# One half of the scan's decay in SBUF, a sixth PSUM bank in the ring, and the feed-forward layer's norms and first weights inside the last attention unit

## What is computed

```python
def _L0_attn_ref(x, ...):
    xn = _ln(x, ln1_w, ln1_b)
    q, k, v = heads of xn @ q_w + q_b, xn @ k_w + k_b, xn @ v_w + v_b     # 16 heads of 8
    attn = softmax(where(causal, q k^T * hd ** -0.5, -inf))
    attn_out = (attn v) @ o_w + o_b
    x_ssm, z = split(xn @ in_proj_w)                                      # 256 channels each
    x_c = silu(conv4(x_ssm) + conv_b)
    dt, Bm, Cm = softplus(x_dbc[..., :R] @ dt_w + dt_b), ...              # 16 states
    h_t = exp(dt_t * A) * h_(t-1) + (x_t * dt_t) * B_t;  y_t = sum_n C_t h_t
    ssm_out = ((y + x_c * D_param) * silu(z)) @ ssm_out_w
    x = x + alpha * attn_out + (1 - alpha) * ssm_out
    h2 = _ln(x, ln2_w, ln2_b)
    return x + gelu(h2 @ ffn_w1 + ffn_b1) @ ffn_w2 + ffn_b2
```

## Time and profile before

| | |
|---|---|
| median of 3 runs | 1673.72 us (1668.92 to 1680.34) |
| the profiled execution | 1669.76 us |
| its span, first to last instruction | 1668.0 us |
| mean granted TensorE clock | 0.934 of full speed |
| PE, DVE, ACT, POOL busy | 84%, 76%, 66%, 52% of the span |
| attention with SSM | 130 to 845 us, then unit 15 alone to 877 |
| norms `ln2` and first weights | 877 to 903 us |
| feed-forward layer | 903 to 961 us |

### The profile page before, as it was taken

How to read it: one execution, slowest core, us unless ns; L and a number is a source line. 1 busy time by engine, 2 the same in 40 slices (tenths; PEclk the granted TensorE clock), 3 DMA queues, 4 the chain that set the end, 5 groups by cost and what they waited for, 6 DMA issues and landing times. The chain is left out here.

```text
span 1668.0 us, 22123 instructions
## 1 busy us (share of the span) xinstructions
PE 1408.5 (84%) x7164; PEld 884.0 (53%) x7164; DVE 1261.6 (76%) x1873; ACT 1093.5 (66%) x1864; POOL 863.4 (52%) x889
## 2 busy tenths in 40 slices
PE   3688898888989898887767887999999999868687
PEld 3234444444444444444324645787786877725573
DVE  2149999989798988989915858687686767848857
ACT  2475668686767778786746736777878788621017
POOL 3137677778696978878843113022222222248843
PEclk9787899999999999999988989999999999979889
DMA  3112222222222222222003010111111111000001
GB/s 90 45 39 83 77 63 78 80 75 70 64 68 67 78 73 68 80 76 75 27 1 95 19 48 26 33 48 45 40 49 39 45 45 45 26 0 1 0 1 50
DMA packets 61688, 84.73 MB, mean 51 GB/s; under 512 B 6621, under 2 KB 32071, under 8 KB 61575
## 3 DMA queue, kind: packets, MB, share of 16 engines
q1 hardware_dynamic: 61474, 83.30, 16.0%
q10 hardware_dynamic: 100, 0.03, 0.0%
HBM read 74.38 MB, written 8.78 MB: 50 GB/s over the span
## 5 line engine op out<-in xcount | busy, mean ns | idle before, releaser
L1760 POOL TENSOR_TENSOR dBx<-dtx,Bb 128x512 f32<-128x512 f32 x256 | 319.6, 1272 | 11.4 <-DMA Bb<-b_dram 10.1
L1355 DVE TENSOR_TENSOR hl<-lsq,hh 128x512 fp32r<-128x512 f32 x320 | 259.5, 821 | 86.7 <-ACT hh L1644 78.9
L1325 DVE TENSOR_TENSOR_SCAN hy<-bank,dBx 128x512 f32<-128x512 f32 x256 | 297.8, 1203 | 10.5 <-ACT bank L1628 6.0
L1641 ACT ACTIVATE lsq<-bank,vcol 128x512 f32<-128x512 f32 x320 | 219.4, 692 | 108.1 <-DVE hl L1355 61.0
L1050 PE MATMUL bank<-QK 127*128 127x128 bf16 (+7 forms) x1024 | 237.7, 318 | 46.6 <-DVE Mx L1315 27.9
L1315 DVE TENSOR_REDUCE Mx<-bank 128x1 f32<-128x384 f32 (+3 forms) x352 | 212.1, 627 | 57.5 <-PE bank L1050 56.7
L1784 POOL TENSOR_TENSOR stage<-stage,lrs 128x512 f32<-128x512 f32 x64 | 92.3, 1443 | 310.5 <-DVE lrs L1435 310.5
L1050 PE MATMUL bank<-x,we1h 128*128 128x512 f32 x640 | 210.7, 411 | 18.8 <-DVE x L1343 9.4
L1569 ACT ACTIVATE PT<-bank 128x512 f32<-128x512 f32 x320 | 183.7, 596 | 52.9 <-PE bank L1050 51.3
L1628 ACT ACTIVATE bank<-dtv,alog 128x512 f32<-128x512 f32 x256 | 170.4, 692 | 61.2 <-DVE hy L1325 60.8
L1050 PEld LDWEIGHTS bank<-QK 127*128 127x128 bf16 (+1 forms) x1024 | 94.3, 104 | 191.9 <-issue 51.5
(11 more groups left out here) (258 smaller groups left out, 2393.6 us busy)
## 6 DMA issues: line engine op xcount, KB each, us to landing
Bb<-b_dram SPq DMA_DIRECT2D x128, 256.0 KB, 3.6
stage<-w_rows SPq DMA_DIRECT2D x64, 256.0 KB, 3.2
parts<-part SPq DMA_DIRECT2D x16, 384.0 KB, 2.7
QK<-parts SPq DMA_DIRECT2D x64, 96.0 KB
QK<-parts SPq DMA_DIRECT2D x64, 64.0 KB
stage<-in_L_ffn_We_dram SPq DMA_DIRECT2D x16, 256.0 KB, 3.3
hy<-in_L_attn_x_dram SPq DMA_DIRECT2D x8, 256.0 KB, 5.8
QK<-parts SPq DMA_DIRECT2D x64, 32.0 KB
```

The source lines that it names most:

```text
L1325: engine.tensor_tensor_scan(hst[:, 2 * (g % 3) + h, :], bank[4 + h][:], dBx[:, g % 4, h, :], 0.0, ALU.mult, ALU.add).then_inc(sems["dve_sc ...
L1355: engine.tensor_tensor(hl[:, sl, :], full[:, f, :], hh[:, sl, :].bitcast(F32), ALU.subtract).then_inc(sems["dve_hl"], 1)
L1641: engine.activation(full[:, f, :], o[:], fn, bias=bias).then_inc(sems["act_up"], 1)
L1760: engine.tensor_tensor(dBx[:, sl, h], dtx[:, b % 2, h], Bb[:, sl], ALU.mult).then_inc(sems["pool_dbx"], 1)
```

## The change

- **Decay.** The decay of half 0 is written to `dec = On[:, 1, :]` in SBUF; half 1 stays in bank 5. The attention's `On` shrinks to one tile, `On[:, 0, :]`, so that `on` of one half batch waits for `wo` of the one before.
- **Ring.** It becomes `[0, 1, 2, 4, 6, 7]`.
- **Accumulation.** `BESIDE` no longer holds for the last batch.
- **Last unit.** `second_norms` and `plan_ffn`, now a generator, are moved on within unit 15 at 16 and 20 steps to its 20. The norm of batch 7 waits until the layer has reached block `LAST_NORM = 4`. The squares of `ln2` go to `part` instead of `lsq`. The first weights and x wait for the end of the SSM branch alone (`ends["ssm"]`); for this the tiles of that branch are allocated first, and the four weight tiles become one, `wall`, with expert 9 in front. The weights of experts 8, 0, 1 and 2 wait for the end of the attention and are split in blocks 2 to 5 (before: 0 to 3).
- **Experts.** In the feed-forward layer `up` takes its banks from the ring and `down` takes 4 and 5. The DVE cast for c = 2 now also holds for e = 9.

```diff
+LAST_NORM = 4
-    ring = [0, 1, 2, 6, 7]
@@ decay, scan
-        it = step("decay", g=g, dt=ssm[b]["dt"], free=[free.get(f"b{4 + h}") for h in range(2)])
+        it = step("decay", g=g, dt=ssm[b]["dt"], free=(free.get("dec"), free.get("b5")))
...
-            free[f"b{4 + h}"] = free[f"dBx{g % 4}{h}"] = it["x"][h]
+            free[("dec", "b5")[h]] = free[f"dBx{g % 4}{h}"] = it["x"][h]
@@ accumulate
-                      y_free=free.get("yT"), y_last=ssm[b]["y"][half], beside=b >= 2 and n in BESIDE, yb_free=free.get(f"yB{half}", nT_read))
+                      y_free=free.get("yT"), y_last=ssm[b]["y"][half], beside=2 <= b < NB - 1 and n in BESIDE, yb_free=free.get(f"yB{half}", nT_read))
@@ plan_mixers
+    def second_norms():
+        for b in range(NB):
+            while ended[b] < 2 or b == NB - 1 and ends.get("ffn", 0) < LAST_NORM:
+                yield
+            k = take()
+            ring.remove(k)
+            finish_norm = p.norm_start((k, ring[0]), (h_last[b],), kind="ln2", b=b, square="part", dst_free=(free.get("yB0"), free.get("yB1")) if b < 2 else None)
+            for _ in range(2):
+                yield
+            r_h2[b] = finish_norm()
+            ring.append(k)
+            yield
...
     for u in range(NU):
-        run_together(attend(u), 20, (mixer, SSM_RATE, False), (tops, 23, False), (prepare(u), 8, True))
+        last = 1 if u == NU - 1 else 0
+        run_together(attend(u), 20, (mixer, SSM_RATE, False), (tops, 23, False), (prepare(u), 8, True),
+                     (seconds, 16 * last, False), (behind_it, 20 * last, False))
+    drain(mixer)
     while late or later:
         settle(0)
-    drain(mixer)
+        next(seconds, None)
+        next(behind_it, None)
+    ends["att"] = tuple(p.last.values())
+    ring.append(3)
+    for _ in behind_it:
+        next(seconds, None)
@@ Experts
+        k = p.first_free(self.ring) if self.ring else c
...
-        if c == 2 and e < 9:
+        if c == 2:
             it["y"] = p.up("dve_hh")
@@ plan_ffn
-    drain(p.norms([(r_h2, b, (bk[b % 4], (h_last[b], *done)), dict(kind="ln2", b=b)) for b in range(NB)]))
-    x.split_weights(0, 9, done)
+    while "ssm" not in ends:
+        yield
+    x.split_weights(0, 9, ends["ssm"])
     load_x(0)
-    x.split(0, r_h2[0], done)
+    while not r_h2[0]:
+        yield
+    x.split(0, r_h2[0], ends["ssm"])
+    while "on" not in ends or 4 not in ring:
+        yield
+    ring.remove(4)
@@ vector_program, scalar_program
-                        engine.tensor_tensor_scan(hst[:, 2 * (g % 3) + h, :], bank[4 + h][:], dBx[:, g % 4, h, :], 0.0,
+                        engine.tensor_tensor_scan(hst[:, 2 * (g % 3) + h, :], bank[5][:] if h else dec, dBx[:, g % 4, h, :], 0.0,
...
-                        engine.activation(bank[4 + h][:], dtv[:, b % 2, h, :], ACT.Exp,
+                        engine.activation(bank[5][:] if h else dec, dtv[:, b % 2, h, :], ACT.Exp,
```

More of the change, by code:

```diff
@@ L244, in normalise @@
         k = take()
-        it = step("on", b=b, g=g, o1=o1, bank=k, free=free.get(f"b{k}"), lrs_free=free.get(f"lrs{hf}"), on_free=free.get(f"On{hf}"))
+        it = step("on", b=b, g=g, o1=o1, bank=k, free=free.get(f"b{k}"), lrs_free=free.get(f"lrs{hf}"), on_free=free.get("On"))
         it["m"] = up("pe_dn")
@@ L462, in mamba @@
         drain(behind)
+        ends["ssm"] = tuple(p.last.values())
     def prepare(u):
@@ L487, in plan_mixers @@
     fetch(0)
[L488 removed]
+    for k in (0, 1, 2, 4):
         ring.remove(k)
     run_together(p.norms(first_norms([(1, 1)] + [(b, l) for l in range(2) for b in range(2, NB)])), 12, (mixer, 5, False))
[L491 removed]
+    ring.extend((0, 1, 2, 4))
     fetch(1)
@@ L507, in __init__ @@
     def __init__(self, p):
-        self.p, self.queue, self.n, self.split_done, self.w_done, self.slots = p, [], 0, {}, {}, {}
+        self.p, self.queue, self.n, self.split_done, self.w_done = p, [], 0, {}, {}
+        self.ring, self.down = None, 6
     def split(self, b, ready, done=()):
@@ L580, in load_x @@
     def load_x(b):
-        it = step("x2load", b=b, free=free.get(f"xin2{b % 2}"), done=done)
+        it = step("x2load", b=b, free=free.get(f"xin2{b % 2}"), done=ends["ssm"])
         l_x2[b] = it["d"] = up(f"x2_in{b % 2}", 16)
+    while "ssm" not in ends:
+        yield
+    x.split_weights(0, 9, ends["ssm"])
     load_x(0)
-    x.split(0, r_h2[0], done)
+    while not r_h2[0]:
[4 more added lines that the diff above has]
+    ring.remove(4)
     for b in range(NB):
+        ends["ffn"] = b
         if b + 1 < NB:
             load_x(b + 1)
-            x.split(b + 1, r_h2[b + 1], done)
-        if b < 4:
-            x.split_weights(b + 1, (8, 0, 1, 2)[b])
-        k = 4 + b % 2
-        it = step("x2tr", b=b, bank=k, free=free.get(f"b{k}"), ready=l_x2[b], done=done)
+            while not r_h2[b + 1]:
+                yield
+            x.split(b + 1, r_h2[b + 1], ends["ssm"])
+        if "att" in ends and split[0] < 4:
+            x.split_weights(split[0] + 1, (8, 0, 1, 2)[split[0]], ends["att"])
+            split[0] += 1
+        k = p.first_free(ring)
+        it = step("x2tr", b=b, bank=k, free=free.get(f"b{k}"), ready=l_x2[b], done=ends["ssm"])
         it["m"] = free[f"xin2{b % 2}"] = up("pe_x2")
         it["x"] = free[f"b{k}"] = r_xT[b] = up("act_x2")
-        drain(x.run(b, 9, ffn_end))
-    drain(x.run(None, None, None))
-    return r_x2
+        yield from x.run(b, 9, ffn_end)
+    yield from x.run(None, None, None)
+    for i in range(split[0], 4):
+        x.split_weights(i + 1, (8, 0, 1, 2)[i], ends["att"])
 def plan_moe(p, x, r_x2, done):
@@ L907, in build @@
             xin = hy[:].rearrange("p a t -> p (a t)").rearrange("p (n c) -> p n c", c=P)
+            Bb = tmp("Bb", [P, 4, T])
+            dtv = tmp("dtv", [P, 2, 2, T])
+            dtx = tmp("dtx", [P, 2, 2, T])
+            dBx = tmp("dBx", [P, 4, 2, T])
+            sp1 = lsq
+            sp2 = tmp("sp2", [P, 2, T])
+            wtap = tmp("wtap", [P, 2, 4, P])
             QK = tmp("QK", [P, 3, 3, 4, T], BF16)
@@ L1041, in norm_args, with square @@
             return xT[:, b, :], hT[:, b, :], mod[:, 1, 4, b:b + 1], mod[:, 1, 3, b:b + 1]
+        def square(it):
+            if it["kind"] == "ln2":
+                return part[:].rearrange("p k t -> p (k t)").bitcast(F32)[:, 0:T]
+            return win if it["kind"] == "ln4" else lsq[:, it["n"] % 2, :]
         def expert_bias(e, c):
@@ L1076, in tensor_program @@
                 elif kind == "ln_b":
-                    sq = win if it["kind"] == "ln4" else lsq[:, it["n"] % 2, :]
+                    sq = square(it)
                     q.wait_ge(it["sq"], it["free1"])
```

78 lines of the change are left out of this document (39 added, 39 removed).

## The result

The changed kernel takes 1695.1 us (median of 4 runs, 1691.75 to 1699.24) against 1671.8 us of the kernel before on the same chip: ratio 1.0132, 95% interval 1.0084 to 1.0180. It is 22 us slower; the forecast was 1690. The profiled execution took 1691.75 us.

A forecast was written before the change was run, and what follows sets the result against it. The prediction took DVE instructions to set the pace of the first half (attention beside SSM). Terms 36 - 12 + 5.7 - 12 = +17.7 us gave 1691.4 on the median of runs, stated as 1690, range 1643 to 1726.

The forecast's parts named there:

- part 1: Half 0's decay in SBUF: 128 scans with two SBUF inputs take turns with POOL, +36 us, bounds 0 and 82.
- part 2: Bank 4 in the ring of six: PE runs one tile further ahead, shortening DVE's waits before maxima, -12 us.
- parts 4 and 5: Last unit and feed-forward layer: first gelu 22 us earlier, layer 64.8 us against 54.7, together -12 us.
- The remainder that a scan meets: Attention beside SSM: a scan starting at random waits 0.42 us for POOL's running instruction; times 128, 54 us of DVE.
- a third was to be swallowed: Of the 54 us of scan delays, a third costs nothing because DVE would wait for PE anyway, leaving +36 us.
- part 3: Last batch without BESIDE: 12 accumulation instructions of 474 ns return to DVE, which has no gap there, +5.7 us.
- between 0 and -47 I take a quarter: Sixth ring bank: of DVE's 47.1 us of waits for PE before maxima, a quarter is saved, -12 us.
- 25.2 us where the unit took 20: Last attention unit: PE needs 14.9 us plus 10.3 for six norms, so +6 us with the waits for squares.
- A: Rival: in the attention a scan takes no turns with POOL and the bank's gain counts in full, 1648 us; chance 0.25.
- C: Rival: scan delays are swallowed by DVE's waits and the sixth bank offsets the rest, 1672 us; chance 0.21.
- B: Rival: POOL, locked out by the scans, becomes the bound and PE and scans wait for it, 1736 us; chance 0.14.
- D: Rival: first gelu waits for weights or last norms, so the end gives nothing, 1702 us; chance 0.06.

The follow-up runs named there:

- run 3: Kernel before with only half 0's decay moved to SBUF, ring left at five banks, bank 4 idle: ratio 1.0250 to the kernel before, +42 us.
- run 2: Kernel before with only half 0's decay in SBUF and bank 4 added to a ring of six: ratio 1.0133 to the kernel before, +22 us.
- run 4: run 2's kernel, but both scans of a pair read half 1's decay in bank 5: ratio 0.9936 to the kernel before, -11 us.
- run 5: Whole changed kernel, but both scans of a pair read half 1's decay in bank 5: ratio 0.9907 to the kernel before, 38 us below the changed kernel.
- run 9: run 2's kernel with POOL computing only half of each dBx product from the fifth state on: ratio 0.9997 to the kernel before.
- run 11: run 2's kernel with eight PT slots and half 1's decay in SBUF too: ratio 1.0592 to the kernel before.
- run 6: Changed kernel with three states of the last batch accumulated by ACT and POOL again: ratio 1.0103 to the kernel before, 4.9 us below the changed kernel.
- run 1: Changed kernel with both decays back in banks 4 and 5 and the ring back at five banks: ratio 1.0022 to the kernel before, +3.7 us.
- run 12: run 8's kernel with the first weights loaded and split behind the norm of batch 0: ratio 0.9959 to the kernel before.
- run 8: run 1's kernel, last batch's BESIDE accumulation restored, batch 6's norm before the first gelu, one shared table for batch 7's: ratio 0.9932 to the kernel before.

## Why the prediction was right

The sign and the mechanism held. That the time came so close (1695 against 1690) is partly luck: the cost of part 1 and the gain of part 2 were taken too small and the gain of parts 4 and 5 too large, and these errors of about +6, -8 and +10 us partly cancel.

- **Part 1, +36 us.** The remainder that a scan meets was worked out as 0.42 us, for one that starts at a random moment; in the changed kernel it is 1557 - 1205 = 0.35 us, 45 us in all; only 72 of the 128 scans met a POOL instruction with more than 0.17 us left. Of the total a third was to be swallowed. That step failed: alone, the part costs 42 us (run 3), where the stretches add up to only 128 x (1483 - 1205) = 36 us, and DVE's waits for PE and ACT there are 65 us (130 to 835), against 59 before. Beside the sixth bank it costs at least 33 (run 2 less run 4), 38 in the whole kernel (run 5), both with the longer wait for ACT on the other side. The two slips, a remainder too large and a swallowing that did not happen, partly cancel. The mechanism was tested from three sides: its removal (runs 4 and 5), half of POOL's work (run 9), and twice the scans (run 11).
- **Part 2, -12 us.** The step "between 0 and -47 I take a quarter" was mis-sized: 20 us (run 3 less run 2, which differ in the ring alone). Run 4 gives 11 without the delays, but pays its own longer wait for ACT, by estimate 9 us, so it does not show that the bank is worth less there. DVE's waits for PE before maxima fall about as far in both: from 47.1 to 27.3 us in run 4, and from 50.3 in run 3 to 27.1 in run 2.
- **Sum of both: +24.** Measured +22 (run 2); the last scan at 861.1 is 25.7 us later, "some 30" with part 3.
- **Part 3, +5.7 us.** Measured 4.9 (run 6).
- **Parts 4 and 5, -12 us.** Mis-sized: -2 (run 1's +3.7 less part 3, give or take 3 by its interval). The layer came out as worked out, 65.0 for 64.8 us. What failed is the step "25.2 us where the unit took 20". The last denominator product should have come 40.4 us after the last scan, and came after 906.8 - 861.1 = 45.7. From there to the first gelu were 6.0 us, not 4.9, for DVE's scale and the norm's own pair stand between. From the last scan to the last denominator product, columns as the earlier trace rows, before and after, and PE's largest wait for POOL's selects after (2.4 us in 2 waits before):

```profile
835.40:869.75 34.35, 24.37 (x168) 10.49 (x169) 6.37 (x13) 17.59 (x33) 15.44 (x31) 0.90 0.00 1
```

```profile
861.10:906.80 45.70, 33.62 (x192) 14.22 (x193) 13.45 (x24) 26.95 (x49) 23.30 (x36) 0.96 0.09 24
```

```profile
PE bank L1101 <- POOL PT L1791: 4.9, 4, 2.1
```

PE's work grew by 9.3 us, near the 10.3 that six norms were priced at. But the forecast let them fill PE's idle time (14.9 + 10.3 of work in a unit of 20, so only 6 us more). They did not: PE is idle 10.0 us of this stretch before and 12.1 after. Part of that is the wait for selects, whose queue on POOL also holds `nT` shifts and an `On` product. Run 12 shows that the weights are not the cause, and the selects alone are not either: in run 8 PE waits only 1.2 us for them in this stretch and is still idle for 10.6. Which wait keeps the gaps open was not tried.
- **Rivals.** A (a scan takes no turns) is refuted by the spread of the `On` scans. C (the delays are swallowed) by run 4 against run 2. B is not the case here, where PE's waits for POOL's selects are 26.4 us from 130 to 870 (13.0 before, 130 to 835) and POOL still has idle time, but it is one scan away (run 11). D (the end gives nothing) is nearly what the end did, for another reason: no wait for weights or last norms, but the last unit's own length.

## What to carry to other kernels

Before an operand is moved from PSUM to SBUF to free a bank, count the DVE instructions that then read two SBUF inputs, and what GpSimd does beside them: here the bank gave 20 us (11 in the run with a longer wait for ACT) and the moved operand took 33 to 42. Both engines' rows show it, as a spread of durations in one direction and the other; bank inputs keep one sharp duration. And where one activation function is interleaved with others, table loads are hardly hidden on a busy ScalarE: move the odd ones ahead of the first, or load one table that serves both.
